# A two-layer graph attention kernel on one core: in a block of the first layer, ScalarE makes the next block's first signs before it normalises

## The reference, cut to what matters

```python
# x: 4096 x 64 float32; adj: 4096 x 4096 int32, 0 or 1
src = h @ a1; dst = h @ a2
e = leaky_relu(src[:, None] + dst[None, :], 0.01)
e = where(adj > 0, e, NEG_INF)
h_prime = softmax(e, axis=1) @ h
...
x = layernorm(x + layer0(x, adj, a))                       # first layer, h = x
x = layernorm(x + layer1(x, adj, weight_w, weight_a, b))   # second: h = x @ weight_w, + bias
```

## Time and profile before

| what | value |
|---|---|
| median of 3 runs | 579.49 us (578.63 to 580.07) |
| profiled execution | 580.5 us, of which its span is 578.7 us |
| busy in the span | PE 453.1, DVE 420.4, ACT 395.0, POOL 164.2 us |
| mean granted TensorE clock | 0.902 of full speed |
| DMA | 87.58 MB, mean 151 GB/s over the span |
| signs on ACT (L513) | 512 instructions, 352.2 us, mean 884 ns |

### The profile page before, as it was taken

One profiled execution on the slowest core, in us unless ns is written; L12 is line 12 of the kernel. 1 busy time (PEld: TensorE's weight loads), 2 busy tenths in 40 slices (PEclk: granted clock), 3 DMA queues, 4 the chain that ended last, 5 costly groups with the idle time before them and its releaser, 6 DMA issues.

```text
span 578.7 us, 11963 instructions
## 1 busy us (share of the span) xinstructions
PE 453.1 (78%) x4356; PEld 418.5 (72%) x4356; DVE 420.4 (73%) x795; ACT 395.0 (68%) x619; POOL 164.2 (28%) x97
## 2 busy tenths in 40 slices
PE   0347579488696987949868875979999989889892
PEld 0226579478595886849857764969999989889791
DVE  0699988859688794968959597928585675848564
ACT  0285386393893939749296537439889898988950
POOL 0547972623616334263443310000010101011010
PEclk9999779979798887988889775979999999999897
DMA  9957899999999999999992300100202012020200
GB/s 201 213 130 204 218 284 273 293 233 297 236 302 257 264 314 225 265 263 264 288 255 78 106 0 1 38 27 11 83 0 82 14 68 82 0 82 0 83 11 10
DMA packets 78875, 87.58 MB, mean 151 GB/s; under 512 B 7424, under 2 KB 74240, under 8 KB 78848
## 3 DMA queue, kind: packets, MB, share of 16 engines
q1 hardware_dynamic: 45056, 53.67, 33.9%
q10 hardware_dynamic: 33792, 33.56, 23.1%
HBM read 77.78 MB, written 9.44 MB: 151 GB/s over the span
## 4 chain that ended last, share of the span: by engine, by line
issue 47%; PE 16%; DVE 16%; POOL 11%; ACT 5%; DMA 2%; SPq 1%; ACTq 1%; POOLq 1%; DVEq 0%
PE acc L397 14%; POOL pos L922 5%; POOL small L893 4%; ACT neg L513 4%; DVE narrow L741 3%; DVE neg L765 2%; DMA acol<-in_L_gnn_a 2%; DVE red L792 2%; DVE turned L753 1%; ACT x1s L528 1%; DVE kept L673 1%; DVE kept L676 1%; PE misc L349 1%; DVE num L795 1%; DVE xy_old L675 1%
## 5 line engine op out<-in xcount | busy, mean ns | idle before, releaser
L513 ACT ACTIVATE neg<-srow,dcol 128x512 int8 (+1 forms) x512 | 352.2, 884 | 15.6 <-issue 9.3
L397 PE MATMUL acc<-xy_old,pos 128*128 128x195 bf16 x1024 | 207.0, 269 | 62.6 <-POOL pos L922 38.6
L397 PE MATMUL acc<-xy_old,neg 128*128 128x195 bf16 x1024 | 206.7, 269 | 0.0
L397 PE MATMUL acc<-stage,pos 128*128 128x195 bf16 x1024 | 184.2, 252 | 13.7 <-DVE red L774 7.0
L397 PE MATMUL acc<-stage,neg 128*128 128x195 bf16 x1024 | 184.1, 253 | 0.0
L397 PEld LDWEIGHTS acc<-xy_old,pos 128*128 128x128 fp8e4 x1024 | 109.9, 107 | 74.5 <-issue 71.7
L397 PEld LDWEIGHTS acc<-stage,pos 128*128 128x128 fp8e4 x1024 | 102.8, 100 | 19.3 <-issue 18.6
L397 PEld LDWEIGHTS acc<-xy_old,neg 128*128 128x128 fp8e4 x1024 | 109.5, 107 | 2.3
L397 PEld LDWEIGHTS acc<-stage,neg 128*128 128x128 fp8e4 x1024 | 102.2, 100 | 0.6
L893 POOL TENSOR_TENSOR small<-small,minus_half 128x4 f32<-128x4 f32 x16 | 31.4, 1963 | 241.9 <-DVE small L813 241.9
L528 ACT ACTIVATE x1s<-num,small 128x64 f32<-128x64 f32 x64 | 22.9, 430 | 101.8 <-POOL small L896 101.8
(11 more groups left out here) (118 smaller groups left out, 322.6 us busy)
## 6 DMA issues: line engine op xcount, KB each, us to landing
stage<-in_adj ACTq DMA_DIRECT2D x64, 512.0 KB, 9.1
stage<-in_adj SPq DMA_DIRECT2D x64, 512.0 KB, 8.3
spill<-turned SPq DMA_DIRECT2D x16, 512.0 KB, 8.0
turned<-spill SPq DMA_DIRECT2D x16, 512.0 KB, 3.7
kept<-in_x SPq DMA_DIRECT2D x8, 128.0 KB, 9.0
out<-x1s SPq DMA_DIRECT2D x8, 128.0 KB, 2.0
kept<-in_L_gnn_a SPq DMA_DIRECT2D x1, 64.0 KB, 11.9
idf<-identity SPq DMA_DIRECT2D x1, 64.0 KB, 11.8
```

The lines of the kernel that those rows point to most:

```text
L397: last = nc.tensor.matmul(acc[:, r, c * XW:(c + 1) * XW], masks[c][:, t // BYTES, t % BYTES, r * P:(r + 1) * P], xy[layer][:, g * GT + t, ...
L513: last = nc.scalar.activation(o[:, t // BYTES, t % BYTES, :], srow[:, bass.ds((s % 2) * 512, 512)], ACT.Sign, bias=dcol[:, layer, col:col ...
```

## The change

In the body of layer 0's blocks on ACT, normalize(s) moves from ahead of copy_wh(s-1), signs(s+2, 0) and load_next(s+2, 0) to behind them. The body is used for the blocks 0 to 5; those of 6 and 7 are written out apart and stay as they are. No instruction is added or removed.

```diff
                 for g in range(1, NG):
                     signs(0, s + 1, g)
                     load_next(s + 1, g)
-                normalize(0, s)
                 if not first:
                     copy_wh(s - 1)
                 signs(0, s + 2, 0)
                 load_next(s + 2, 0)
+                normalize(0, s)
                 copy_x1(s)
```

## The result

The changed kernel takes 588.88 us (median of 4 runs, 587.58 to 590.95), the one before 579.78 in the same comparison. The ratio is 1.0156 with an interval of 1.0111 to 1.0202: slower by 9 us. Measured a second time it was 1.0141 (1.0115 to 1.0166), so 8.2 us (0.0141 of 580) is the better figure. Its interval is 6.7 to 9.6 us. The forecast was 7.1 us slower, 586.6.

What follows compares the result with a forecast made beforehand. The prediction took the chain looping through POOL's queue as the bound, not busy engines or loads; five blocks at 1.1 us plus block 0 at 1.6 added 7.1 to 579.5, giving 586.6 us, with an 8-in-10 range of 579.8 to 590.5.

Steps and rivals of the forecast that it cites:

- What bounds the kernel: Layer 0, blocks 0 to 5: a chain in a loop sets the period, with the normalisation in it through POOL's queue.
- The sentence that the loads don't matter: Loads don't set the period: DVE waited for a landing only once between 110 and 290 us, for 1.5 us.
- Part 1: ACT's signs and copy go ahead: DVE's 4.05 us stall at granule 0's mask moves to the reads, gain zero.
- Part 2: ACT's normalisation behind the DMA issues begins 0.8 to 1.0 us late, absorbed because residual waits for DVE's narrowing anyway.
- as the text forecast (1.4): Sign that the forecast is right: ACT's normalisation begins about 1.4 us behind the first narrowing.
- Part 3: DVE's granule 0 mask runs between POOL's residual and positive mask, making the latter 1.1 us late a block; bounds 0 and 1.5.
- the 3.4 that was named as the sign: Sign that the forecast is right: POOL's positive mask behind residual takes 3.4 us or more instead of 2.35.
- Block 0: Residual falls behind the narrowing, so POOL's positive mask ends 1.6 us late; bounds 0.4 and 2.0.
- The sum: Five blocks at 1.1 us and block 0 at 1.6 make 7.1 us slower.
- A sign that failed: Sign that the forecast is right: PE's wait for POOL grows by about 1.1 us a block.
- The deviation named in the prediction: POOL's power, shut out by DVE's mask and narrowing, took 3.29 us without pushing the narrowing back; at most 0.1 us a block.

Runs made afterwards that it cites:

- the kernel with the issues behind: The changed kernel with the normalisation ahead of the two DMA issues, still behind the signs and the copy: 587.7 us, ratio 1.0112.
- three kernels as fast as the one before: Changed kernel with DVE's granule-0 mask behind granule 1's transposition, 581.6 us; kernel before with that swap, 580.93 us; kernel before with load issues ahead of normalisation, 580.98 us.

## Why the prediction was right, point by point

- **What bounds the kernel** held: the loop through POOL's queue. Taking the positive mask out from behind residual gave 11.4 us at once, and DVE's wait for the signs could be made longer (4.96 us) or taken away without a gain or loss of its own. The sentence that the loads don't matter rested on one profile, though: in others of equally fast kernels a late landing costs 1.0 us in block 1, and once in block 4 too.
- **Part 1**, the early signs cost nothing and give nothing. Held: they ended at 222.23, 1.5 us ahead of the narrowing that gates the issue, and DVE's freed wait came back at the reads. It holds for POOL's old order alone.
- **Part 2**, the normalisation 0.8 to 1.0 us late and the delay absorbed. It came 1.36 us behind the first narrowing, as the text forecast (1.4), against 0.56 before, so 0.8 late. It was absorbed in the blocks 2 to 5, but not in 0 and 1, where the second narrowing waits for a landing: by the kernel with the issues behind, 2 us in all were paid (the difference of the table's rows in these two blocks is 1.6 in the first profile and 2.3 in the second). The prediction had no such term for block 1.
- **Part 3**, the mask's turn at 1.1 us a block. Mechanism and order held to the instruction. The size is 0.98 to 1.0 in the blocks 2 to 4 and 0.96 to 1.0 in block 5, some 0.1 below. The positive mask took 3.34 us, just short of the 3.4 that was named as the sign.
- **Block 0** was put at 1.6 us late; the profiles show 0.4 and 1.2, for the second narrowing began at another place relative to the first than in the one profile that I had.
- **The sum**: 6.5 and 7.2 us in the measured distances against 7.1, by a smaller block 0 and a larger block 1. The measured ratio stands for 8.2 us. From block 0's statistics to block 6's the changed kernel takes 221.1 and 222.9 us and the one before 213.9; three kernels as fast as the one before take 213.8, 214.4 and 215.8. So the loss is there, where it was forecast. How it divides is less sure. These three have 61.9, 63.1 and 62.0 us as the sum of their six distances, the kernel before 60.8, and against them the changed kernel's 67.3 and 68.0 are only 4.2 to 6.2 us more. The blocks 2 to 5 give 4.0 us; 1 to 4 us of the 8.2 aren't settled. That 7.1 came so near owes something to luck: 1.0 us of block 1's excess is the landing, while block 0 fell 0.4 to 1.2 short of its 1.6.
- **A sign that failed**: I wrote that PE's wait for POOL grows by 1.1 us a block. In block 3 it grew only from 4.10 to 4.28 us. Rows of PE before the change, then after:

```profile
223.50 0.32 PE L397 MATMUL acc<-xy_old,pos 128*128 128x195 bf16 x1 [4.10 <-POOL pos L922]
```

```profile
226.69 0.60 PE L409 MATMUL flip<-idf,x1s 128*64 128x128 f32 x4 [0.83 <-ACT x1s L528]
...
231.56 0.32 PE L397 MATMUL acc<-xy_old,pos 128*128 128x195 bf16 x1 [4.28 <-POOL pos L922]
```

The later normalisation moved PE's transposition (L409) too. Before the change PE didn't wait for it in this block; now it waits 0.83 us for ACT. The two waits together grew by the 1.0 us of the mask's turn. Over the whole stretch PE's wait for ACT at the transposition grew from 4.8 to 10.6 us.

The Trainium skill's rule on the shared pair ("SBUF — State Buffer", Who interferes with whom) is borne out where one instruction of DVE and one of POOL overlap: a mask of 1.22 us took 2.78 behind a positive mask. The deviation named in the prediction is there again: POOL's power begins under a mask and lasts to the end of the narrowing behind it (220.50 + 3.29 = 223.79, against 223.75), while the narrowing keeps 2.29 us. So the taking of turns isn't without exception either: the power was there before the narrowing and didn't delay it.

## What to carry to other kernels

Before you remove a wait, ask what the waiting engine will do next and which other engine it shuts out while doing so: a wait that costs nothing can keep the way free for an instruction that does count. Look in the queue of the engine that is late for an instruction that stands ahead only by its place; moving that one was worth more than any wait, and it turned the same edit from a loss of 8 us into a gain of some 13. An edit's worth belongs to the order around it, so try it again once the loop has been changed.

## What the runs showed of the hardware

- VectorE's two-input mask and GpSimd's residual and positive mask exclude each other, and if both wait they alternate. A mask of 1.22 us took 1.75 behind residual, and 2.78 behind a positive mask that had begun 0.66 us earlier. GpSimd's small power doesn't fit: it began 0.96 us ahead of a narrowing, ended with it, and the narrowing kept 2.29 us.
- A transposition on VectorE doesn't hold GpSimd up: the positive mask kept 2.36 us with one over its start (224.10 to 225.35).
- A DMA share of 1.02 with 273 GB/s wasn't a limit: the same kind of transfers ran at 298 GB/s at a share of 1.04.
- A landing 1.2 us earlier in the first granules changed which of the two engines went first (narrowing 79.10, positive mask 79.66, against 80.32 and 79.38), and PE's granule behind it began 2.3 us later.
